# One run of transposes, contexts and scores per slot in a float32 encoder layer

## The reference

```python
q, k, v = split_heads(x @ wq + bq), split_heads(x @ wk + bk), split_heads(x @ wv + bv)
attn = softmax(q @ k.T * 48 ** -0.5 + adj[:, None])
x1 = rmsnorm(x + (attn @ v) @ wo + bo, alpha1, gamma1)       # alpha * x / rms + gamma
x2 = rmsnorm(x1 + silu(x1 @ w1 + b1) @ w2 + b2, alpha2, gamma2)   # w1: 384 x 1536
out = layernorm(x + x2)
```

## Time and profile before

| | |
|---|---|
| time, median of 3 runs | 2931.57 us (2929.22 to 2931.73) |
| the profiled execution | 2935.65 us, its span 2933.9 us |
| PE busy | 2906.3 us (99%), 25216 matmuls |
| PE weight loads | 2856.3 us (97%) |
| DVE, ACT, POOL busy | 1970.4 us (67%), 1439.3 us (49%), 708.2 us (24%) |
| granted TensorE clock | 0.998 of full over the span |
| DMA | 171.93 MB, 59 GB/s on average |
| chain of work that ended last | PE 95%, DVE 2%, ACT 1% |

### The profile page before, as it was taken

One profiled execution on the slowest core, in us unless ns is written; L12 is line 12 of the kernel. 1 busy time (PEld: TensorE's weight loads), 2 busy tenths in 40 slices (PEclk: granted clock), 3 DMA queues, 4 the chain that ended last, 5 costly groups with the idle time before them and its releaser, 6 DMA issues.

```text
span 2933.9 us, 62758 instructions
## 1 busy us (share of the span) xinstructions
PE 2906.3 (99%) x25216; PEld 2856.3 (97%) x25216; DVE 1970.4 (67%) x3621; ACT 1439.3 (49%) x4260; POOL 708.2 (24%) x968
## 2 busy tenths in 40 slices
PE   7999999999999999999999999999999999999998
PEld 7999999999999999999999999999999999999998
DVE  6766667666666676666666666666666666676666
ACT  5545455454454554545544545455454454554543
POOL 1222222222222222222222222222222222222222
PEclk9999999999999999999999999999999999999999
DMA  6221211211212112112121121121211212112110
GB/s 172 68 69 40 64 57 48 69 52 53 69 36 69 56 48 70 49 55 69 36 69 56 48 69 47 58 61 44 69 54 51 69 40 64 57 48 69 49 43 28
DMA packets 155491, 171.93 MB, mean 59 GB/s; under 512 B 18624, under 2 KB 155200, under 8 KB 155200
## 3 DMA queue, kind: packets, MB, share of 16 engines
q1 hardware_dynamic: 151952, 166.92, 18.9%
q10 hardware_dynamic: 3248, 0.99, 0.2%
HBM read 92.35 MB, written 25.17 MB: 40 GB/s over the span
## 4 chain that ended last, share of the span: by engine, by line
PE 95%; DVE 2%; ACT 1%; issue 0%; DMA 0%; POOL 0%; ACTq 0%; POOLq 0%; DVEq 0%
PE ps_work L454 47%; PE ps_rows L524 27%; PE ps_rows L454 7%; PE ps_att L466 4%; PE ps_att L475 4%; PE ps_att L486 2%; PE ps_att L490 2%; PE ps_work L566 2%; PE ps_rows L566 1%; ACT probs L712 1%; DVE w_s L879 0%; DVE h L961 0%; DMA stage<-in_L_gnn_wq 0%; DVE neg_max L891 0%; DVE probs L887 0%
## 5 line engine op out<-in xcount | busy, mean ns | idle before, releaser
L454 PE MATMUL ps_work<-x1T,w_s 128*128 128x256 f32 x6912 | 835.4, 282 | 0.7 <-ACT h_raw L768 0.6
L454 PEld LDWEIGHTS ps_work<-x1T,w_s 128*128 128x128 f32 x6912 | 823.9, 189 | 1.1 <-ACT h_raw L768 0.8
L524 PE MATMUL ps_rows<-w_s,h 128*128 128x384 f32 x4608 | 816.9, 338 | 0.0
L524 PEld LDWEIGHTS ps_rows<-w_s,h 128*128 128x128 f32 x4608 | 796.1, 188 | 7.5
L768 ACT ACTIVATE h_raw<-ps_work,b_col 128x256 f32<-128x256 f32 x768 | 322.1, 471 | 463.0 <-PE ps_work L454 457.4
L712 ACT ACTIVATE probs<-probs,neg_max 128x128 f32<-128x128 f32 x1024 | 396.0, 388 | 239.5 <-DVE neg_max L891 239.5
L961 DVE TENSOR_TENSOR h<-h_raw,h 128x512 fp32r<-128x512 f32 x384 | 359.1, 935 | 13.2
L959 DVE CAST h<-h_raw 128x512 fp32r<-128x512 f32 x384 | 165.2, 430 | 294.6 <-ACT h_raw L768 294.6
L411 POOL TENSOR_SCALAR mean_sq<-sum_sq 128x1 f32<-128x1 f32 x256 | 92.3, 361 | 955.9 <-ACT squares L727 955.8
L423 POOL TENSOR_TENSOR x_last<-x_last,rows 128x768 f32<-128x768 f32 x64 | 117.3, 1834 | 748.9 <-PE ps_att L466 748.9
L454 PE MATMUL ps_work<-wv_s,xT 128*128 128x384 f32 x1152 | 232.6, 347 | 3.3 <-ACT qk_flat L748 2.4
(11 more groups left out here) (86 smaller groups left out, 3423.6 us busy)
## 6 DMA issues: line engine op xcount, KB each, us to landing
qk<-qk_flat SPq DMA_DIRECT2D x381, 96.0 KB, 2.3
x_in<-in_x SPq DMA_DIRECT2D x64, 384.0 KB, 3.3
x_res<-in_x SPq DMA_DIRECT2D x64, 384.0 KB, 3.9
x_last<-in_x SPq DMA_DIRECT2D x64, 384.0 KB, 3.1
out<-y SPq DMA_DIRECT2D x63, 384.0 KB, 2.5
bias<-in_adj SPq DMA_DIRECT2D x64, 128.0 KB, 3.8
qk<-qk_flat SPq DMA_DIRECT2D x127, 64.0 KB, 2.0
qk<-qk_flat SPq DMA_DIRECT2D x127, 32.0 KB, 2.0
```

Of the source, the lines that this page charges most:

```text
L454: mm = pe.matmul(ps_out, stationary(sta), moving(mov), start=(i == 0), stop=(i == n - 1))
L524: mm = pe.matmul(ps_rows[b][:, 0:d], h[:, sta, m, b * P:(b + 1) * P], w2_s[:, mov, m, :], start=(m == 0 and i == 0), stop=(m == fc - 1 and ...
```

## The change

- The lags shrink: slot `t` now transposes and projects pair `t`, makes the scores of pair `t-1`, contexts and output of `t-2`, and both up and down of `t-3`. There are 67 slots and one that only ends the last pair. The branches `starting` and `ending` go.
- On PE the slot begins with 28 transpositions (`x`: 6, probabilities of graph 0: 8, `x1`: 6, probabilities of graph 1: 8), then the contexts of graph 0 and 1, then the scores of graph 0 and 1, and then all products with weights in one stretch: output, queries and keys, values, up, down.
- The contexts go to `ps_rows[b]` in place of `ps_att[b]`, so that the scores can follow them at once; they wait only for `probsT_ready[b]`.
- `v_first` and `v_rest` hold the values of two pairs. `x_res` is gone: `x_in` is loaded a second time in each slot for the residual, after its transposition. `bias` holds one pair.
- The orders on ACT, DVE, POOL and SP are written anew to fit. The exponentials of graph 0 come before the query copies, those of graph 1 behind them. `keys_out` stands behind both `norm1` on DVE. The splitting of the weights is spread over the first slots in another way.

```diff
             def slot_program(t):
+                g_scores, g_attn, g_ff = t - LAG_SCORES, t - LAG_ATTN, t - LAG_FF
+                if live(t):
+                    transpose_x(t)
+                if live(g_attn):
+                    transpose_probs(g_attn, 0)
+                if live(g_ff) and g_ff < last:
+                    transpose_x1(g_ff)
+                if live(g_attn):
+                    transpose_probs(g_attn, 1)
                     for b in range(PAIR):
                         context(g_attn, b)
+                if live(g_scores):
+                    for b in range(PAIR):
+                        scores(g_scores, b)
+                if live(g_attn):
+                    if g_attn == 0:
                         pe.wait_ge(weight_split, out_units)
                     for b in range(PAIR):
                         output_product(g_attn, b)
                 if live(t):
+                    project_qk(t)
+                    for b in range(PAIR):
+                        project_v(t, b)
+                if live(g_ff):
+                    if g_ff == 0:
+                        pe.wait_ge(weight_split, up_units)
+                    up(g_ff)
+                    if g_ff == last - 1:
+                        transpose_x1(last)
+                    for b in range(PAIR):
+                        down(g_ff, b)
```

The order on ACT:

```diff
+                if live(t):
+                    transposed_hi(t, 0, ps_work[1], xT_done, xT, xT_hi)
+                    transposed_hi(t, 1, ps_rows[0], xT_done, xT, xT_hi)
...
+                if live(g_attn):
+                    probsT_out(g_attn, 0)
+                if live(g_ff) and g_ff < last:
+                    transposed_hi(g_ff, 1, x1_third(g_ff), x1T_done, x1T, x1T_hi)
+                if live(g_attn):
+                    probsT_out(g_attn, 1)
+                    context_hi(g_attn, 0)
+                if live(g_ff) and g_ff < last:
+                    transposed_hi(g_ff, 0, x1_first(g_ff), x1T_done, x1T, x1T_hi)
+                if live(g_attn):
+                    context_hi(g_attn, 1)
+                if live(g_out):
+                    output_squares(g_out, 1)
...
+                if live(g_scores):
+                    exponentials(g_scores, 0)
+                if live(g_attn):
+                    attention_squares(g_attn, 0)
+                if live(t) and t > 1:
+                    queries_out(t, 0)
+                if live(g_attn):
+                    attention_squares(g_attn, 1)
+                if live(t):
+                    queries_out(t, 1)
+                if live(g_scores):
+                    exponentials(g_scores, 1)
...
+                if live(g_ff):
+                    act.preload_act_table(ACT.Silu)
...
+                    silu(g_ff)
```

And on DVE, from the scores on:

```diff
+                if live(g_scores):
+                    bias_and_max(g_scores, 0)
+                if live(g_attn):
+                    residual1(g_attn, 0)
+                if live(g_scores):
+                    bias_and_max(g_scores, 1)
+                if live(g_attn):
+                    residual1(g_attn, 1)
+                weights_lo(t, "softmax")
+                if live(g_out):
+                    if g_out < last:
+                        layer_norm(g_out, 0)
+                    norm2_and_stats(g_out, 1)
+                if live(g_attn):
+                    for b in range(PAIR):
+                        norm1(g_attn, b)
+                if live(t):
+                    keys_out(t)
+                if live(g_scores):
+                    normalise(g_scores, 0, 0)
+                if live(t):
+                    values_out(t, 0)
```

More of the change, by code:

```diff
@@ L62, in build_layer @@
     scale = float(dh) ** -0.5
-    slots = groups + LAG_FF2
+    slots = groups + LAG_FF
+    last = groups - 1
     assert nodes == P and kd * P == d and HEADS == 8 and 2 * rest == TILE and dh <= HALF
@@ L300, in through, with x1_first @@
             return (g + 1) * each
[L302 to L308, removed]
+        def x1_first(g):
+            return ps_work[0][:, 0:2 * toks] if g < last else ps_att[0][:, 0:2 * toks]
         def x1_third(g):
-            return ps_work[1] if ending(g + LAG_FF1) else ps_rows[1]
+            return ps_rows[1][:, 0:toks] if g < last else ps_att[0][:, 2 * toks:3 * toks]
         def run_slots(slot):
-            for t in range(slots):
-                slot(t, t % 2)
+            for t in range(slots + 1):
+                slot(t)
         def group_rows(ap, g):
@@ L373, in slot_program @@
-                if live(g_ff2) and t < slots - 1:
+                    sp.dma_start(x_last[:], group_rows(x, g_ff)).then_inc(x_last_loaded, 16)
+                if live(t):
+                    if live(t - 1):
+                        sp.wait_ge(scores_done[PAIR - 1], through(t - 1))
+                    for i in range(3):
+                        sp.wait_ge(qk_ready[i], through(t))
+                    for p0, c, to, pair, n in moves if t > 0 else moves[:len(moves) // 2]:
+                        sp.dma_start(qk[to:to + n, :, pair, :], qk_flat[p0:p0 + n, :, c, :]).then_inc(qk_moved, 16)
@@ L381, in slot_program @@
[L381 to L386, removed]
-                        sp.dma_start(qk[to:to + n, :, pair, :], qk_flat[p0:p0 + n, :, c, :]).then_inc(qk_moved, 16)
-                for n in loads_due.get((t, 1), ()):
+                        sp.wait_ge(y_ready[b], through(g_out))
@@ L389, in slot_program @@
+                        sp.dma_start(out[g_out * PAIR + b], y[:, b, :]).then_inc(y_stored, 16)
+                for n in loads_due.get((t, 1), ()) if t > 0 else ():
                     load_weights(n)
@@ L1090, in slot_program @@
                     transposed_lo(t, 1, ps_rows[0], xT_hi, xT, xT_lo)
[L1091 removed]
                 if t == 0:
+                    weights_lo(t, "keys")
                     scale_query_bias()
[L1094 to L1099 removed]
+                    weights_lo(t, "values")
@@ new lines, in slot_program @@
+                if live(g_scores):
+                    for half in range(2):
+                        normalise(g_scores, 1, half)
+                weights_lo(t, "end")
+                if live(g_ff):
+                    for m in range(fc // 2):
+                        split_h(g_ff, m)
+                        weights_lo(t, m)
+                    if g_ff == last - 1:
+                        transposed_lo(last, 1, x1_third(last), x1T_hi, x1T, x1T_lo)
+                        transposed_lo(last, 0, x1_first(last), x1T_hi, x1T, x1T_lo)
+                    residual2(g_ff, 0)
+                    norm2_and_stats(g_ff, 0)
+                    if g_ff == last:
+                        layer_norm(g_ff, 0)
```

737 lines of the change are left out of this document (272 added, 465 removed).

## The result

The change makes the kernel slower: 2948.49 us (median of 4 runs, 2946.78 to 2949.99) against 2931.65 us (4 runs, 2929.22 to 2932.84), a ratio of 1.0059 with a 95% interval of 1.0047 to 1.0071. The profiled execution has a span of 2947.3 us, 13.4 us longer than before. The forecast was +9.6 on the span and 2941 us.

The account below looks back on a forecast made before the run. PE bounds the kernel, busy 2906.3 of 2933.9 us. Slots +5.3, start -2 and end +6.3 make +9.6 on the span; added to the median of 2931.57 this gives 2941 us, range 2925 to 2958.

Parts of the forecast that it names:

- The pause: Before graph 1's contexts, PE waits for ACT's probability copy: 0.28 us plus 0.02 restart, 0.30 per slot.
- The changes of division: PE's array in each slot: three changes instead of four, 0.52 us instead of 0.74; contexts to scores taken at 0.20.
- The slot: Steady slot on PE: 0.30 us of new wait against 0.22 less for changes of division, +0.088 per slot.
- the 45.3 to 45.4 that the prediction named as its sign: Steady slots: a length of 45.3 to 45.4 us would show the forecast right, below 45.2 wrong.
- The other covers: Other possible PE waits in a steady slot: all covered, graph 1's values (`keys_out`) by 0.2 us, query copies by 1.0.
- The rival of a late `keys_out`: DVE's chain ahead of graph 1's values comes late: 2947 to 2965 us, middle 2956; chance 0.20.
- The ends: First slots and pipeline end together: start -2 us with an error of 3, end +6.3.
- The one idle stretch of slot 64: Up product in slot 64: PE idles 3.7 us once, waiting for the first silu behind both graphs' exponentials.
- The slow clock behind it: After slot 64's idle stretch: the clock falls as in an earlier 3.2 us idle stretch, costing 3.4 us.
- the rest of the end: End of the kernel apart from slot 64's idle stretch and slow clock: shorter by 0.9 us.
- the start, counted as -2: First slots, slow for weights, their splitting and first `qk` DMAs: 1 to 2 us less, counted -2, error 3.
- The clock: Rival: transpositions, contexts and scores, together 7.3 us, bring the clock down in each slot: +204 us, 3145; chance 0.03.

Follow-up runs that it names:

- The split scores: Changed kernel with scores and output product alternating graph by graph on PE, two changes of division more per slot: 2972.96 us.
- the second trace of before: The kernel before, unchanged, profiled and timed once more: 2938.34 us in that run, beside 2939.62 of the same kernel.
- the second set: Later set of runs with both kernels unchanged: changed kernel 2949.07 us against 2939.62 of the kernel before, ratio 1.0032.
- the extra operation: Changed kernel with one unused DVE maximum over 384 columns straight ahead of `keys_out`: 2959.47 us.
- the fastest version: Changed kernel with x1 and x transpositions moved, w2 splits later, and in slot 64 both graphs' exponentials behind the silus, normalisings before the residual: 2911.8 us.
- the late exponentials alone: Changed kernel with only graph 1's exponentials and normalising in slot 64 moved behind the silus and split copies: 2947.14 us.
- the second experiment: Changed kernel with four transpositions of the next pair's x moved from the slot's start to between up and down: 2938.11 us.

## Why the prediction was right, step by step

**The pause.** Forecast 0.28 us plus 0.02 for the restart; the two graphs' blocks are 0.29 further apart with it than without it (0.72 against 0.43), and taking the cause away shortens contexts to scores by 0.31. The copy's path was forecast at 1.38 from the last transposition and takes that: the last of graph 1's eight starts at 1524.55, ACT's copy at 1524.86, the contexts of graph 1 at 1525.93. This step held.

**The changes of division.** Contexts to scores had no row before. Now the scores' first pair starts 0.55 behind the last block of strips, whose four groups take 0.44 by their own pace, so 0.11, and 0.10 more until the second pair: 0.21 against the 0.20 taken. The split scores give 0.20 for each of two others. The Trainium skill, TensorEngine Tiling (Array Packing), Key Properties, says that changing the tiling mode drains TensorE; a price at each change tried agrees with that.

**The slot.** Forecast +0.088, measured +0.156, so the slots cost 9.2 us for 5.3. The slots of 45.42 and 45.43 us lie just outside the 45.3 to 45.4 that the prediction named as its sign. The mechanism was right, and up to the scores every position in the slot came out within 0.01 us of the forecast. What was mis-sized are the terms behind it, which partly cancel, all from one assumption: that matmuls that aren't changed keep their pace. The forecast kept down at the pace that it had behind the scores, 12.48 without the change of division; it takes 12.72, +0.24. It kept up at 12.83; it takes 12.67, -0.16. The output product takes 3.24 on average for 3.29. This is what the text called "the matmuls stay the same in number and shape, so I count only the changes of division": true, and not enough, since the same matmuls went up to 2% faster or slower in the new order. Two of the experiments tie down's pace to what stands ahead of it; for up no edit tries it, and that its new place is the reason is an inference. Against the second trace of before, whose up blocks are slower, the same slot is only 0.09 to 0.10 longer, and the second set's loss is 9.5 us; that both come close to the forecast is chance.

**The other covers.** `keys_out` was forecast to start at 17.2 after the first transposition and starts at 17.1; its slack is 0.32 for a forecast 0.2. Neither values nor query copies wait in a steady slot. The rival of a late `keys_out` didn't come, and the extra operation shows that it wasn't far: each tenth beyond 0.32 goes to PE.

**The ends.** Forecast +4.3 in all, measured +4.2, and that is luck, as two errors cancel. The one idle stretch of slot 64 is there, 3.73 us for 3.7. The slow clock behind it cost less than the forecast took from slot 0: the 72 matmuls behind it take 10.16 us for 8.45, so 1.7 against 3.4. If the rest of the end is 0.9 shorter as forecast, which I didn't measure by itself, the end cost 4.5 for a forecast 6.3, and the start, counted as -2, came out at about -0.3, inside its error of 3. The waits of slot 3 (0.91, 0.47 and 1.69 us) were no term of the forecast; the kernel before has waits of the same kind in its slots 3 and 4, the longest 1.88 and 1.12.

**The clock.** It didn't fall in the slots. The windows of a steady slot, columns as above, of the transpositions and then of the contexts and scores:

```profile
1521.60:1524.70 3.10, 3.10 (x29) 2.98 (x27) 1.62 (x4) 2.17 (x4) 0.00 (x0) 1.00 0.33 98
1524.70:1529.00 4.30, 4.20 (x99) 3.56 (x97) 2.96 (x5) 3.00 (x6) 2.56 (x3) 1.00 0.06 23
```

The clock stays at 2.4 GHz through 7.4 us of transpositions, contexts and scores. The Trainium skill, TensorE: Matmul & The Clock Gate, Part 4, holds that transposes don't count as busy in the same way. Here 3.1 us of transpositions alone, followed by contexts and scores, didn't bring the clock down; a longer run of nothing but transpositions stands in no trace, so these runs don't decide on the rule.

Of the 7.5 us between 2941 and 2948.5, 3.9 are the slots (9.2 for 5.3) and next to nothing the ends, which makes 13.4 of 9.6 on the span. The other 3.4 to 3.8 are the spread of single executions: the profiled one of before was 4.1 above the median of its runs, that of after 0.6.

## What to carry to other kernels

Where PE is the bound, put work that its other engines must answer far enough ahead of its reader. Here the whole path, from the start of the last transposition over the copy to the contexts, takes 1.38 us, and PE had 1.1 us of its own in between: gathering like with like saved some 0.2 us of changes and opened a pause of 0.3, and four transpositions moved by one place closed it. Then read the blocks from start to start before and after, those too that weren't edited, since their pace may move with their neighbours. At the ends of a pipeline, order each engine by what PE needs next, for the order of the steady slots isn't right where half of the stages are empty.

## What the runs showed of the hardware

- A stretch of equal matmuls has more than one steady pace at full clock: 173.3 or 176.7 ns with 384 columns, and 117.3 ns, 118 to 119 or 120.0 with 256. Up blocks of 12.67 us have 117.3 throughout; those of the kernel before, 12.88, 13.00 and 13.12 us with a slower start and a change of division in them, end at 117, 119 and 120. In a steady slot, straight after up, down took the slow one, behind transpositions or behind scores the fast one. Slot 64 doesn't fit: there down comes straight after up too and takes 12.49 us, the fast pace, in the changed kernel, and the same again in the fastest version, but 12.72 with the late exponentials alone. For the products behind the scores both paces were seen with the same instructions ahead (the query product 3.20 and 3.17 us in two neighbouring slots of the second experiment), and so were all three of the up blocks before. What settles the pace beyond that is open.
- The mix of such paces isn't the same in every trace of one kernel: the up product of the kernel before has slots of 45.27 us on average in one trace and 45.33 in another. Its whole time was 2931.65 us in the first set, 2929.99 on a second chip, 2940.07 on a third and 2939.62 on a fourth, one set each; that it is the chip which makes the difference isn't shown. The changed kernel took 2948.5 and 2949.1. A ratio of less than half a per cent that is measured in one set can have this in it.
- A change of the array's division costs about 0.2 us: 0.20 for scores to product and back, 0.21 for contexts to scores, 0.22 for contexts to product. Into the contexts the rows show 0.12.
- After an idle stretch of 3.7 us in the middle of full load, the granted clock was 0.55 of 2.4 GHz over 3.8 us and then 1.00, and the 72 matmuls behind it cost 1.7 us more. In another run the same idle stretch cost 2.7.
